# Expert products on 64x64 tiles of the array, with the expert weights loaded in an earlier phase

## The chip, the cores and the metric

The kernel runs on one core of a Trainium2 chip, as one program. The metric is the device time of one execution in microseconds (us), the median of the runs that were timed. All data are float32. The engines are named as in the profile: PE (TensorE matmul), PEld (TensorE weight load), DVE (VectorE), ACT (ScalarE), POOL (GpSimd) and SP (SyncE, which here only issues DMAs).

## The reference, cut to what matters

The model first runs a Fourier operator on 128 images of 64 x 64 (four layers; this takes the first two thirds of the span), joins 32 text rows to each, and goes on with a batch B = 128 of T = 96 tokens of D = 64 features. An attention with a recurrent state follows, and then a mixture of experts, which is what the change is about:

```
shared = gelu(x @ W1s + b1s) @ W2s + b2s
rw     = softmax(x @ Wr);  topw, topi = top_k(rw, 2);  topw /= sum(topw)
mask   = sum(one_hot(topi, 8) * topw)                 # weight of each expert for each token, mostly 0
h      = gelu(einsum('bsd,edf->bsef', x, W1p) + b1p)  # 8 experts, 64 -> 256
priv   = einsum('bsef,efd->bsed', h, W2p) + b2p       # 256 -> 64
out    = h_in + shared + einsum('bsed,bse->bsd', priv, mask)
```

The kernel computes all 8 experts for all tokens and multiplies each hidden value by its expert's weight before the second product, so that the second products of the shared expert and of the 8 private ones add up in one sum. The biases b2s and b2p have been added to `h2` by the phase before.

## The kernel before

The program is a row of phases, each with its own block of instruction streams, one for every engine, and a barrier of all engines behind it (`end_phase`, L244). `tokens` (L2132) calls them in this order: `token_norm_phase`, `update_phase`, `decay_phase`, `attention_phase`, `gate_phase`, `expert_phase`. Inside a phase the engines are ordered by semaphores alone, and each engine runs its own list in the order written. No planner sets the order.

`update_phase` (L1391) computes, for 16 groups of 8 batch entries, relu(e @ Dx.T) and its sums over channels; PE, ACT and DVE work, and SP has nothing to do until all sums are there (L1488), when it stores them.

`expert_phase` (L1955) takes the 12288 tokens in 32 blocks of 4 batch entries, that is 384 tokens (`CT`). Features or hidden units stand on the partitions, tokens along the free axis. Expert 0 is the shared one, experts 1 to 8 are the private ones. The lists of the engines:

- SP (L1992) loads W1 (the same weights twice, on partitions 0 to 63 and 64 to 127) and two copies of a 64 x 64 unit matrix. Then for each block i, two blocks ahead of its use (two buffers): the input `et` twice (L2008, the same 64 rows on both halves of the partitions; the buffer is free when block i - 2 has made its last hidden product), the mask (L2011: 8 rows of 384 weights, each broadcast to all 128 partitions, 1.5 MB; free when block i - 2 has made its last masked multiplication), and the store of block i - 2 (L2003).
- ACT (L2023) loads W2 and the two biases b1 by 11 DMAs, waits for them, and then takes the gelu with bias of 18 tiles a block (two for each of the 9 experts, 128 hidden units x 384 tokens) from four PSUM buffers `ps_h` into a ring of six SBUF tiles `ht`.
- DVE (L2045) multiplies the 16 tiles of the private experts by their mask, in place. Behind tile 6 of a block (the first of expert 3) it copies the finished sum of the block before out of PSUM (`totals`, L2047), behind tile 10 it adds the turned result to `h2` (`rows`, L2052).
- PE (L2077) makes, for each expert e, `hidden` (L2078): two products of 64 x 128 weights with the 384 tokens, one on each half of the rows of the array; and `outputs` (L2089), two experts later: two products of 128 x 64 weights, one on each half of the columns of the array, whose sums stay in PSUM over all 9 experts (upper and lower 64 partitions hold one half of the hidden units each). So hidden(e) and outputs(e - 2) take turns. Behind outputs(2) of the next block comes `turn` (L2102): four products with the unit matrices that add the two halves and turn the sum to tokens on partitions.

In float32 each matmul is two weight loads and two matmul records of the profile. `hidden` waits for ACT two experts back, `outputs` for DVE, `turn` for `totals`; such a wait stands on the first weight load behind it.

Of the kernel before, what the change touches and what calls it, by code (L numbers as in the profile page):

```python
# [12 lines left out]
P = 128  # L13
# [8 lines left out]
CH = 512  # L22
# [1367 lines left out]

def update_phase(nc, sems, W, usum):  # L1391

# [3 lines left out]
    with ExitStack() as ctx:  # L1396
# [557 lines left out]

def expert_phase(nc, sems, W, d, out, e2t_dram, gates):  # L1955

# [12 lines left out]
    n, CT = B // NB, NB * T  # L1969
    F = 2 * P  # L1970
    TILES = 2 * (E + 1)
    with ExitStack() as ctx:
        def sb(name, shape, dt=F32):
            return ctx.enter_context(nc.sbuf_tensor("x_" + name, shape, dt))

        w1 = sb("w1", [P, E + 1, F])
        w2 = sb("w2", [P, E + 1, 2, D])
        b1 = sb("b1", [P, E + 1, 2])
# [4 lines left out]
        units = sb("units", [P, D])  # L1983
# [8 lines left out]
        def _(eng):  # L1992
            for half in range(2):
                rows = slice(D * half, D * half + D)
                eng.dma_start(w1[rows, 0, :], d["W1s"]).then_inc(s.w_in, 16)
                eng.dma_start(w1[rows, 1:, :], d["W1p"].rearrange("e d f -> d e f")).then_inc(s.w_in, 16)
            for half in range(2):
                eng.dma_start(units[D * half:D * half + D, :], d["eye"][0:D, 0:D]).then_inc(s.const_in, 16)
            ov = out.rearrange("(n b) t d -> n t b d", b=NB)
# [22 lines left out]
        @block.scalar  # L2022
        def _(act):  # L2023
            act.dma_start(w2[:, 0], d["W2s"].rearrange("(t p) d -> p t d", p=P)).then_inc(s.w_tmp, 16)  # L2024
            for e in range(E):
                act.dma_start(w2[:, 1 + e], d["W2p"][e].rearrange("(t p) d -> p t d", p=P)).then_inc(s.w_tmp, 16)  # L2026
            with nc.allow_non_contiguous_dma("biases to partitions"):
                act.dma_start(b1[:, 0, :], d["b1s"].rearrange("(t p) -> p t", p=P)).then_inc(s.w_tmp, 16)  # L2028
                act.dma_start(b1[:, 1:, :].rearrange("p e t -> p (e t)"),
                              d["b1p"].rearrange("e (t p) -> p (e t)", p=P)).then_inc(s.w_tmp, 16)  # L2030
            act.wait_ge(s.w_tmp, 16 * 11)
# [12 lines left out]
        @block.vector  # L2044
        def _(dve):  # L2045
            ve = nc.vector
            def totals(i, par):  # L2047
                dve.wait_ge(s.fx_done, (E + 1) * (i + 1))
                at_least(dve, s.um_done, i)
                ve.tensor_copy(total[:, :], ps_e[par][:, 0:CT]).then_inc(s.s_ready, 1)  # L2050

            def rows(i, par, r):  # L2052
                dve.wait_ge(s.um_done, i + 1)
                if not (isinstance(i, int) and i < 2):
                    dve.wait_ge(o_out[par], 16 * r)
                ve.tensor_tensor(res[:, par], W["h2"][:, bass.ds(NB * i, NB), :],  # L2056
                                 ps_r[:, 0:NB * D].rearrange("p (b d) -> p b d", b=NB), ALU.add).then_inc(s.uo_ready, 1)

# [18 lines left out]
        def _(pe):  # L2077
            def hidden(i, par, r, e):  # L2078
# [3 lines left out]
                if not (isinstance(i, int) and i == 0 and e < 2):  # L2082
                    pe.wait_ge(s.a_ready, t - 2)
                for half in range(2):
                    rows = slice(D * half, D * half + D)
                    nc.tensor.matmul(ps_h[(2 * par + 2 * e + half) % 4][:, 0:CT], w1[rows, e, P * half:P * half + P],  # L2086
                                     et[rows, par, :], start=True, stop=True).then_inc(s.fy_done, 1)

            def outputs(i, par, e):  # L2089

                if e == 0:
                    pe.wait_ge(s.a_ready, TILES * i + 2)
                    at_least(pe, s.s_ready, i - 1)
                else:
                    pe.wait_ge(s.t_ready, 2 * E * i + 2 * e)
                for half in range(2):
                    ins = nc.tensor.matmul(ps_e[par][D * half:D * half + D, 0:CT], w2[:, e, half, :],  # L2097
                                           ht[:, (2 * e + half) % 6, :], start=(e == 0), stop=(e == E),
                                           skip_group_check=True)
                ins.then_inc(s.fx_done, 1)  # L2100

            def turn(i):  # L2102
                pe.wait_ge(s.s_ready, i + 1)
                at_least(pe, s.uo_ready, i)
                for b in range(NB):
                    ins = nc.tensor.matmul(ps_r[:, D * b:D * b + D], total[:, T * b:T * b + T], units[:, :],  # L2106
                                           start=True, stop=True)
                ins.then_inc(s.um_done, 1)

            def body(i, par, r, last):  # L2110

                later = not (isinstance(i, int) and i == 0)
                for e in range(E + 1):
# [5 lines left out]
                    if e == 4 and later:  # L2119
                        turn(i - 1)  # L2120
                if last:
                    outputs(i, par, E - 1)
                    outputs(i, par, E)
                    turn(i)

            pe.wait_ge(s.w_tmp, 16 * 11)
            pe.wait_ge(s.w_in, 64)
            pe.wait_ge(s.const_in, 32)
            walk(pe, n, body)


def tokens(nc, ctx, sems, d, h_img, out):  # L2132
# [12 lines left out]
    W = {"gate": sb("gate", [T, B, 8]), "Wr": sb("Wr", [D, 8]), "eye": sb("eye", [P, P]), "h2": sb("h2", [T, B, D])}  # L2145
    W["e"] = W["h2"]
    with nc.Block() as block:
        @block.sync
# [5 lines left out]
    with ExitStack() as c:  # L2154
# [4 lines left out]
        W["x"] = sb("x", [P, 2, B * T], c)  # L2159
        update_phase(nc, sems, W, usum)  # L2160
        end_phase(nc, sems)
# [5 lines left out]
    end_phase(nc, sems)  # L2167
    expert_phase(nc, sems, W, d, out, e2t_dram, gates)
    end_phase(nc, sems)
# [35 lines left out]
```

## Time and profile before

| | us |
|---|---|
| median of 3 runs | 3385.28 (3376.81 to 3389.48) |
| span of the profiled execution, first to last instruction | 3381.9 |
| PE busy | 2785.4 (82%) |
| DVE busy | 2119.0 (63%) |
| ACT busy | 1400.7 (41%) |
| POOL busy | 638.6 (19%) |

The profile gives the one profiled execution by its span; which of the three times was taken nearest to it, it does not say. The busy shares are means over stages of different kinds. The expert phase is the last one: it begins at about 2842 us of the span and runs to its end, some 540 us, 16% of the whole. Times in rows are us from the start of the span. A group of rows of the timeline gives start, length, engine, line, operation, names and shapes, and how many instructions have been merged; a PE shape of 64*128 is a weight tile of 64 rows and 128 columns of the array.

### The profile page before, as it was taken

To read this page: it belongs to the slowest core of one execution; us is meant where nothing else is said; L and a number is where in the kernel's file an instruction comes from. 1 tells how busy PE (TensorE), PEld (TensorE's weight loads), DVE (VectorE), ACT (ScalarE), POOL (GpSimd) and SP (SyncE) were. 2 spreads that over 40 slices of the span, in tenths; PEclk is the share of its full clock that TensorE was granted. 3 is DMA by queue.
4 is the path that set the end of the run, shared out by engine and by line. 5 is a ranking of instruction groups with operands and counts; after the bars stand their busy time and mean duration, and the time that the engine had idled before them with its cause. 6 is when DMAs were issued, how large, how long until landed. Compare 5 with 4: busy or idle time off the path is not lost. (4 is left out here: it accounts for less than half of the span.)

```text
span 3381.9 us, 104377 instructions
## 1 busy us (share of the span) xinstructions
PE 2785.4 (82%) x45316; PEld 1477.3 (44%) x45316; DVE 2119.0 (63%) x3067; ACT 1400.7 (41%) x2298; POOL 638.6 (19%) x806
## 2 busy tenths in 40 slices
PE   3589999988999999699999975825488852999999
PEld 1245555544555555355555531202266640333333
DVE  4567777766787777667777761035467653555555
ACT  2545555545555555445555541011011110666665
POOL 3003332110233311014341100000145520000000
PEclk9779989888999999899999997967777766999999
DMA  5066666654888887288888745951122203566775
GB/s 164 18 153 147 142 139 145 139 138 128 264 266 259 249 253 201 93 269 256 253 258 257 242 143 218 430 140 38 54 62 65 67 18 68 96 120 119 120 120 91
DMA packets 243990, 541.22 MB, mean 160 GB/s; under 512 B 77857, under 2 KB 124705, under 8 KB 229953
## 3 DMA queue, kind: packets, MB, share of 16 engines
q1 hardware_dynamic: 229664, 527.43, 56.8%
q10 hardware_dynamic: 13920, 7.72, 1.1%
q8 instruction: 336, 5.51, 0.6%
q14 instruction: 70, 0.57, 0.1%
HBM read 320.28 MB, written 214.78 MB: 158 GB/s over the span
## 5 line engine op out<-in xcount | busy, mean ns | idle before, releaser
L838 ACT ACTIVATE p_v<-p_ps,k_scale_bias 128x1024 f32<-128x1024 f32 x384 | 446.6, 1201 | 635.3 <-PE p_ps L947 635.1
L707 DVE STREAM_TRANSPOSE p_t<-p_ps 128x1024 f32<-128x1024 f32 x192 | 363.7, 1968 | 305.8 <-PE p_ps L700 305.4
L822 POOL COPY k_xm<-p_sp 64x288 f32<-64x288 f32 x384 | 268.8, 700 | 1453.4 <-DVE p_sp L301 1436.7
L947 PEld LDWEIGHTS p_ps<-k_idfty,p_t 64*128 64x128 f32 x6144 | 403.6, 206 | 182.5 <-issue 182.5
L845 ACT ACTIVATE p_ps<-p_ps 128x1024 f32<-128x1024 f32 x384 | 388.3, 1011 | 168.3 <-PE p_ps L963 167.9
L947 PE MATMUL p_ps<-k_idfty,p_t 64*128 64x128 f32 x6144 | 445.8, 299 | 14.7 <-issue 14.7
L291 DVE STREAM_TRANSPOSE p_vt<-p_v 128x1024 f32<-128x1024 f32 x384 | 448.2, 1208 | 0.0
L2065 DVE TENSOR_TENSOR x_ht<-x_ht,x_mask 128x384 f32<-128x384 f32 x512 | 268.6, 556 | 247.2 <-ACT x_ht L2039 244.2
L2039 ACT ACTIVATE x_ht<-x_ph,x_b 128x384 f32<-128x384 f32 x576 | 303.3, 578 | 195.3 <-PE x_ph L2086 195.3
L938 PE MATMUL p_ps<-p_v,k_wbd 32*32 32x512 f32 x4096 | 298.2, 607 | 21.7 <-DVE p_t L707 10.4
L2086 PE MATMUL x_ph<-x_et,x_w 64*128 64x384 f32 x1152 | 266.3, 540 | 35.7 <-DMA x_b<-in_L_ffn_b1p_dram 34.5
L2097 PE MATMUL x_pe<-x_ht,x_w 128*64 128x384 f32 x1152 | 249.9, 513 | 0.3 <-DVE x_ht L2065 0.3
L963 PE MATMUL p_ps<-p_v,k_wbd 32*32 32x512 f32 x6144 | 239.7, 602 | 11.0 <-DVE p_sp L301 1.1
L296 DVE STREAM_TRANSPOSE p_at<-p_ps 128x1024 f32<-128x1024 f32 x192 | 224.7, 1209 | 31.3 <-PE p_ps L269 31.3
L269 PE MATMUL p_ps<-p_vt,k_dfty 32*32 32x512 f32 x6144 | 227.9, 602 | 18.0 <-ACT p_v L838 4.6
L280 PE MATMUL p_ps<-p_at,k_dftx 32*64 32x192 f32 x6144 | 174.1, 349 | 21.6 <-DVE p_at L296 15.5
L2086 PEld LDWEIGHTS x_ph<-x_et,x_w 64*128 64x128 f32 x1152 | 87.7, 186 | 192.9 <-ACT x_ht L2039 153.1
L700 PE MATMUL p_ps<-p_yt,k_idftx 64*64 64x192 f32 x3072 | 152.8, 338 | 10.8 <-DVE p_yt L719 10.8
L938 PEld LDWEIGHTS p_ps<-p_v,k_wbd 32*32 32x32 f32 x4096 | 75.4, 103 | 193.4 <-issue 83.3
L938 PE MATMUL p_ps<-p_v,k_pwbd 4*32 4x512 f32 x2048 | 148.6, 610 | 10.1 <-issue 8.7
L301 DVE STREAM_TRANSPOSE p_sp<-p_ps 128x768 f32<-128x768 f32 x96 | 94.4, 983 | 95.8 <-PE p_ps L280 95.8
L280 PEld LDWEIGHTS p_ps<-p_at,k_dftx 32*64 32x64 f32 x6144 | 129.9, 141 | 49.9 <-issue 36.6
(298 smaller groups left out, 3114.3 us busy)
## 6 DMA issues: line engine op xcount, KB each, us to landing
field<-p_v SPq DMA_DIRECT2D x768, 256.0 KB, 4.6
p_v<-field SPq DMA_DIRECT2D x64, 2048.0 KB
x_mask<-expert_weights SPq DMA_DIRECT2D x32, 1536.0 KB, 13.9
l_v<-field SPq DMA_DIRECT2D x16, 2048.0 KB, 25.9
k_xm<-field SPq DMA_DIRECT2D x12, 2048.0 KB, 24.7
k_mixw<-in_L_tok_fw_dram SPq DMA_DIRECT2D x16, 1152.0 KB, 10.4
at_cf<-state_coefficients SPq DMA_DIRECT2D x32, 384.0 KB
k_mixw<-field SPq DMA_DIRECT2D x4, 2048.0 KB, 23.7
```

Of the source, the lines that this page charges most:

```text
L280: ins = nc.tensor.matmul(ps[64 * j:64 * j + 64, g, 0:6 * C], K["dftx"][rows, s, t, :], at[rows, s, :, 16 * t + 6 * j:16 * t + 6 * j + 6], ...
L291: return nc.vector.transpose(cols(vt), cols(px.rearrange("p (g m) -> p g m", g=G)))
L707: return nc.vector.transpose(st[:, q].rearrange("p x c -> p c x"), ps[:, 2 * q:2 * q + 2, :].rearrange("p j (m c) -> p c j m", c=C))
L822: nc.gpsimd.tensor_copy(view[64 * k:64 * k + 64, :, j, :, G * i:G * i + G], sp[64 * j:64 * j + 64, :, :, 16 * k:16 * k + M1].rearrange("p ...
L838: nc.scalar.activation(field[:, 2 * q:2 * q + 2, CH * half:CH * half + CH], ps[:, e, 2 * q:2 * q + 2, :], ACT.Relu, bias=bias, scale=scale ...
L845: nc.scalar.activation(ps[:, e, 2 * q:2 * q + 2, :], ps[:, e, 2 * q:2 * q + 2, :], ACT.Square, accum_out=K["zs"][:, at:at + 1]).then_inc(s ...
L938: nc.tensor.matmul(ps[C * a:C * a + C, e, g, :], weights[rows, C * g:C * g + C], v[rows, b, col:col + CH], start=True, stop=False, skip_gr ...
L947: ins = nc.tensor.matmul(ps[:, e, 2 * q + h, col:col + 128], lines, K["idfty"][rows, :], start=False, stop=True, skip_group_check=True)
L2039: nc.scalar.activation(ht[:, j % 6, :], ps_h[(2 * par + j) % 4][:, 0:CT], ACT.Gelu, bias=b1[:, j // 2, j % 2:j % 2 + 1]).then_inc(s.a_read ...
L2065: ve.tensor_tensor(h, h, mask[:, par, j // 2 - 1, :], ALU.mult).then_inc(s.t_ready, 1)
L2086: nc.tensor.matmul(ps_h[(2 * par + 2 * e + half) % 4][:, 0:CT], w1[rows, e, P * half:P * half + P], et[rows, par, :], start=True, stop=Tru ...
L2097: ins = nc.tensor.matmul(ps_e[par][D * half:D * half + D, 0:CT], w2[:, e, half, :], ht[:, (2 * e + half) % 6, :], start=(e == 0), stop=(e ...
```

## The change

The hidden products are cut once more, in their 128 output columns: four products of 64 x 64 weights per expert, each on its own quarter of the array. The second products are cut once more in their 128 contracted rows: again four products of 64 x 64 weights, with the two row halves summed apart, in two PSUM banks (`ps_e[:, par, c]`, c = 0 and 1). DVE's `totals` adds the two sums by one more operation. The turned result goes into the last 128 columns of the same banks, so `ps_r` is gone, and its reuse is guarded by `uo_ready` in `outputs`. The waits of `hidden` and `outputs` now stand on a `nop` ahead of the products. The loads of W1, the units, W2 and the biases have moved to SP in `update_phase`, as 17 DMAs ahead of its wait; ACT issues none.

```diff
+def expert_weights(nc, eng, X, d, done):
+    for half in range(2):
+        rows = slice(D * half, D * half + D)
+        eng.dma_start(X["w1"][rows, 0, :], d["W1s"]).then_inc(done, 16)
+        eng.dma_start(X["w1"][rows, 1:, :], d["W1p"].rearrange("e d f -> d e f")).then_inc(done, 16)
+        eng.dma_start(X["units"][rows, :], d["eye"][0:D, 0:D]).then_inc(done, 16)
+    eng.dma_start(X["w2"][:, 0], d["W2s"].rearrange("(t p) d -> p t d", p=P)).then_inc(done, 16)
+    for e in range(E):
+        eng.dma_start(X["w2"][:, 1 + e], d["W2p"][e].rearrange("(t p) d -> p t d", p=P)).then_inc(done, 16)
...
@@ update_phase, block.sync @@
+            loaded = expert_weights(nc, eng, X, d, s.w_in)
             eng.wait_ge(s.sp_ready, n // 2)
...
             eng.wait_ge(s.y_out0, 64)
+            eng.wait_ge(s.w_in, loaded)
@@ expert_phase @@
-        ps_e = [ctx.enter_context(nc.psum_tensor(f"x_pe{b}", [P, CH], F32)) for b in range(2)]
-        ps_r = ctx.enter_context(nc.psum_tensor("x_pr", [T, CH], F32))
+        ps_e = ctx.enter_context(nc.psum_tensor("x_pe", [P, 2, 2, CH], F32))
             def totals(i, par):
-                ve.tensor_copy(total[:, :], ps_e[par][:, 0:CT]).then_inc(s.s_ready, 1)
+                ve.tensor_copy(total[:, :], ps_e[:, par, 0, 0:CT]).then_inc(s.tt_done, 1)
+                dve.wait_ge(s.tt_done, i + 1)
+                ve.tensor_tensor(total[:, :], total[:, :], ps_e[:, par, 1, 0:CT], ALU.add).then_inc(s.s_ready, 1)
             def hidden(i, par, r, e):
-                for half in range(2):
-                    rows = slice(D * half, D * half + D)
-                    nc.tensor.matmul(ps_h[(2 * par + 2 * e + half) % 4][:, 0:CT], w1[rows, e, P * half:P * half + P],
-                                     et[rows, par, :], start=True, stop=True).then_inc(s.fy_done, 1)
+                pe.nop(nofuse=True)
+                for c in range(2):
+                    for half in range(2):
+                        rows, at = slice(D * half, D * half + D), P * half + D * c
+                        ins = nc.tensor.matmul(ps_h[(2 * par + 2 * e + half) % 4][D * c:D * c + D, 0:CT], w1[rows, e, at:at + D],
+                                               et[rows, par, :], start=True, stop=True)
+                        if c == 1:
+                            ins.then_inc(s.fy_done, 1)
             def outputs(i, par, e):
-                    at_least(pe, s.s_ready, i - 1)
+                    at_least(pe, s.uo_ready, i - 1)
...
+                pe.nop(nofuse=True)
                 for half in range(2):
-                    ins = nc.tensor.matmul(ps_e[par][D * half:D * half + D, 0:CT], w2[:, e, half, :],
-                                           ht[:, (2 * e + half) % 6, :], start=(e == 0), stop=(e == E),
-                                           skip_group_check=True)
+                    for c in range(2):
+                        rows = slice(D * c, D * c + D)
+                        ins = nc.tensor.matmul(ps_e[D * half:D * half + D, par, c, 0:CT], w2[rows, e, half, :],
+                                               ht[rows, (2 * e + half) % 6, :], start=(e == 0), stop=(e == E),
+                                               skip_group_check=True)
```

## Rows read from the trace of the kernel before

**Rows 1.** The page, part 4: the chain that ended last, by line.
```profile
PE x_ph L2086 7%; PE x_pe L2097 7%; PE x_pr L2106 1%; DMA x_b<-in_L_ffn_b1p_dram 1%; ACTq L2026 0%; ACT x_ht L2039 0%; ACT L2039 0%; DVE x_ht L2065 0%; ACTq L2028 0%; DVE x_total L2050 0%; ACTq L2024 0%; DVE x_res L2056 0%
```
**Rows 2.** Busy us (and instructions) of each engine, clock, DMA share, GB/s; expert phase.
```profile
2890.00:3370.00 480.00, 480.00 (x2465) 161.44 (x2464) 277.46 (x553) 291.66 (x555) 0.00 (x0) 1.00 0.67 117
```
**Rows 3.** Timeline of two stretches within a block of the expert phase.
```profile
3100.90 0.56 DVE L2065 TENSOR_TENSOR x_ht<-x_ht,x_mask 128x384 f32<-128x384 f32 x1 [0.69 <-ACT x_ht L2039]
...
3101.37 0.55 DVE L2050 COPY x_total<-x_pe 128x384 f32<-128x384 f32 x1
...
3102.54 0.89 PE L2106 MATMUL x_pr<-x_units,x_total 128*96 128x64 f32 x8
...
3103.36 0.92 PE L2086 MATMUL x_ph<-x_et,x_w 64*128 64x384 f32 x4
...
3106.64 0.92 PE L2086 MATMUL x_ph<-x_et,x_w 64*128 64x384 f32 x4
...
3107.49 0.87 PE L2097 MATMUL x_pe<-x_ht,x_w 128*64 128x384 f32 x4
3107.67 1.05 ACT L2039 ACTIVATE x_ht<-x_ph,x_b 128x384 f32<-128x384 f32 x2 [0.59 <-PE x_ph L2086]
3108.28 1.03 DVE L2065 TENSOR_TENSOR x_ht<-x_ht,x_mask 128x384 f32<-128x384 f32 x2 [0.61 <-ACT x_ht L2039]
...
3108.29 0.92 PE L2086 MATMUL x_ph<-x_et,x_w 64*128 64x384 f32 x4
```
**Rows 4.** PE's timeline: the turn of the next block.
```profile
3118.14 0.89 PE L2106 MATMUL x_pr<-x_units,x_total 128*96 128x64 f32 x8
```
**Rows 5.** Groups by line, 2890 to 3370: count, busy us, mean ns, idle before and releaser.
```profile
L2039 ACT ACTIVATE x_ht<-x_ph,x_b 128x384 f32<-128x384 f32 x555 | 292.4, 578 | 188.3 <-PE x_ph L2086 188.3
L2065 DVE TENSOR_TENSOR x_ht<-x_ht,x_mask 128x384 f32<-128x384 f32 x492 | 258.2, 556 | 201.8 <-ACT x_ht L2039 198.8
...
L2050 DVE COPY x_total<-x_pe 128x384 f32<-128x384 f32 x31 | 17.1, 551 | 0.0
```
**Rows 6.** Timeline, the last products: two `outputs` with nothing between them.
```profile
3374.28 1.51 PE L2097 MATMUL x_pe<-x_ht,x_w 128*64 128x384 f32 x8
```
**Rows 7.** Timeline of an image layer: 64x64 tiles, four at once.
```profile
1909.90 1.18 PEld L700 LDWEIGHTS p_ps<-p_yt,k_idftx 64*64 64x64 f32 x32
1909.90 1.53 PE L700 MATMUL p_ps<-p_yt,k_idftx 64*64 64x192 f32 x32
```
**Rows 8.** PE's timeline of an image layer: two groups of one shape, a nop between.
```profile
1913.28 0.59 PE L938 MATMUL p_ps<-p_v,k_wbd 32*32 32x512 f32 x1
1913.30 0.69 PE L269 MATMUL p_ps<-p_vt,k_dfty 32*32 32x512 f32 x7
```
**Rows 9.** As rows 2: a block's stream, then the phase's start.
```profile
3110.40:3125.00 14.60, 14.60 (x78) 4.94 (x76) 8.56 (x18) 8.52 (x17) 0.00 (x0) 1.00 0.64 128
...
2853.00:2863.00 10.00, 0.00 (x0) 0.00 (x0) 0.00 (x0) 0.00 (x0) 0.00 (x0) 0.50 0.76 195
2863.00:2873.50 10.50, 0.00 (x0) 0.00 (x0) 0.00 (x0) 0.00 (x0) 0.00 (x0) 0.50 0.79 132
```
**Rows 10.** Line L2011, the mask's DMA: last line of its view.
```profile
DMA to landing us min/median/max: 13.2/13.9/24.1
```
**Rows 11.** The chain that ended last, at the expert phase's start.
```profile
2842.38 0.46 ACTq L2024
...
2848.32 25.43 DMA x_b<-in_L_ffn_b1p_dram
```
**Rows 12.** Timeline at the start: first masked multiplications, outputs of expert 1.
```profile
2878.46 1.03 DVE L2065 TENSOR_TENSOR x_ht<-x_ht,x_mask 128x384 f32<-128x384 f32 x2 [37.85 <-ACT x_ht L2039]
...
2882.57 0.87 PE L2097 MATMUL x_pe<-x_ht,x_w 128*64 128x384 f32 x4
```
**Rows 13.** As rows 2: within the update phase.
```profile
2320.00:2370.00 50.00, 42.08 (x231) 18.07 (x230) 19.94 (x41) 10.46 (x24) 0.00 (x0) 0.94 0.00 1
```
**Rows 14.** Timeline: SP's first work in the update phase.
```profile
2388.55 2.81 SPq L1493 DMA_DIRECT2D update_sums<-up_row  x4
```

More of the change, by code:

```diff
@@ L1388, in _, with update_phase @@
                 dve.sem_inc(s.aggr, 1)
-def update_phase(nc, sems, W, usum):
+def expert_weights(nc, eng, X, d, done):
+    D = d["Wr"].shape[0]
+    E = X["w1"].shape[1] - 1
+    for half in range(2):
[6 more added lines that the diff above has]
+        eng.dma_start(X["w2"][:, 1 + e], d["W2p"][e].rearrange("(t p) d -> p t d", p=P)).then_inc(done, 16)
+    with nc.allow_non_contiguous_dma("biases to partitions"):
+        eng.dma_start(X["b1"][:, 0, :], d["b1s"].rearrange("(t p) -> p t", p=P)).then_inc(done, 16)
+        eng.dma_start(X["b1"][:, 1:, :].rearrange("p e t -> p (e t)"), d["b1p"].rearrange("e (t p) -> p (e t)", p=P)).then_inc(done, 16)
+    return 16 * (6 + 1 + E + 2)
+def update_phase(nc, sems, W, X, d, usum):
     s = sems
@@ L1952, in _, with expert_phase @@
                         .then_inc(s.st_done, 1)
-def expert_phase(nc, sems, W, d, out, e2t_dram, gates):
+def expert_phase(nc, sems, W, X, out, e2t_dram, gates):
     s = sems
@@ L1974, in sb @@
             return ctx.enter_context(nc.sbuf_tensor("x_" + name, shape, dt))
-        w1 = sb("w1", [P, E + 1, F])
-        w2 = sb("w2", [P, E + 1, 2, D])
-        b1 = sb("b1", [P, E + 1, 2])
+        w1, w2, b1, units = X["w1"], X["w2"], X["b1"], X["units"]
         et = sb("et", [P, 2, CT])
@@ L1992, in _ @@
         def _(eng):
-            for half in range(2):
-                rows = slice(D * half, D * half + D)
[L1995 to L1998, printed above, removed]
             ov = out.rearrange("(n b) t d -> n t b d", b=NB)
@@ L2023, in _ @@
         def _(act):
[L2024 to L2031, printed above, removed]
             def body(i, par, r, last):
@@ L2055, in rows @@
                     dve.wait_ge(o_out[par], 16 * r)
-                ve.tensor_tensor(res[:, par], W["h2"][:, bass.ds(NB * i, NB), :],
-                                 ps_r[:, 0:NB * D].rearrange("p (b d) -> p b d", b=NB), ALU.add).then_inc(s.uo_ready, 1)
+                ve.tensor_tensor(res[:, par].rearrange("p (c b) d -> p c b d", c=2),
+                                 W["h2"][:, bass.ds(NB * i, NB), :].rearrange("p (c b) d -> p c b d", c=2),
+                                 ps_e[0:T, par, :, CT:].rearrange("p c (b d) -> p c b d", d=D), ALU.add).then_inc(s.uo_ready, 1)
             def body(i, par, r, last):
@@ L2083, in hidden @@
                     pe.wait_ge(s.a_ready, t - 2)
-                for half in range(2):
-                    rows = slice(D * half, D * half + D)
-                    nc.tensor.matmul(ps_h[(2 * par + 2 * e + half) % 4][:, 0:CT], w1[rows, e, P * half:P * half + P],
-                                     et[rows, par, :], start=True, stop=True).then_inc(s.fy_done, 1)
+                pe.nop(nofuse=True)
[6 more added lines that the diff above has]
+                            ins.then_inc(s.fy_done, 1)
             def outputs(i, par, e):
@@ L2092, in outputs, with turn @@
                     pe.wait_ge(s.a_ready, TILES * i + 2)
-                    at_least(pe, s.s_ready, i - 1)
+                    at_least(pe, s.uo_ready, i - 1)
                 else:
                     pe.wait_ge(s.t_ready, 2 * E * i + 2 * e)
+                pe.nop(nofuse=True)
                 for half in range(2):
-                    ins = nc.tensor.matmul(ps_e[par][D * half:D * half + D, 0:CT], w2[:, e, half, :],
-                                           ht[:, (2 * e + half) % 6, :], start=(e == 0), stop=(e == E),
-                                           skip_group_check=True)
+                    for c in range(2):
[3 more added lines that the diff above has]
+                                               skip_group_check=True)
                 ins.then_inc(s.fx_done, 1)
-            def turn(i):
+            def turn(i, par):
                 pe.wait_ge(s.s_ready, i + 1)
-                at_least(pe, s.uo_ready, i)
                 for b in range(NB):
-                    ins = nc.tensor.matmul(ps_r[:, D * b:D * b + D], total[:, T * b:T * b + T], units[:, :],
+                    ins = nc.tensor.matmul(ps_e[0:T, par, b // 2, CT + D * (b % 2):CT + D * (b % 2) + D], total[:, T * b:T * b + T], units[:, :],
                                            start=True, stop=True)
@@ L2119, in body @@
                     if e == 4 and later:
-                        turn(i - 1)
+                        turn(i - 1, 1 - par)
                 if last:
@@ L2123, in body @@
                     outputs(i, par, E)
[L2124 to L2128, printed above, removed]
+                    turn(i, par)
             walk(pe, n, body)
@@ L2146, in tokens @@
     W["e"] = W["h2"]
+    E, F = d["W1p"].shape[0], d["W1p"].shape[2]
+    X = {"w1": sb("w1", [P, E + 1, F]), "w2": sb("w2", [P, E + 1, 2, D]), "b1": sb("b1", [P, E + 1, 2]), "units": sb("units", [P, D])}
     with nc.Block() as block:
@@ L2159, in tokens @@
         W["x"] = sb("x", [P, 2, B * T], c)
-        update_phase(nc, sems, W, usum)
+        update_phase(nc, sems, W, X, d, usum)
         end_phase(nc, sems)
@@ L2167, in tokens @@
     end_phase(nc, sems)
-    expert_phase(nc, sems, W, d, out, e2t_dram, gates)
+    expert_phase(nc, sems, W, X, out, e2t_dram, gates)
     end_phase(nc, sems)
```

2 lines of the change are left out of this document (removed).

## The prediction

> **What bounds the kernel now.** I read the chain of waits first: the end of the program hangs on PE's two expert products, with 7% of the span each, the turn with 1%, and 1% of waiting for the bias DMA [rows 1]. Then the busy times by stretch: from 2890 to 3370 us PE is busy in all 480.00 us, at full clock, ACT in 292, DVE in 277, the DMA engines in 0.67 [rows 2]. So this phase is PE's, and the timeline says how it is spent: a `hidden` starts at 3106.64, the `outputs` behind it at 3107.49, the next `hidden` at 3108.29, that is 0.85 + 0.80 = 1.65 us an expert; a turn takes 3103.36 - 3102.54 = 0.82 us [rows 3]. From turn to turn it is 15.60 us [rows 3, 4], and 9 x 1.65 + 0.82 = 15.7 gives that within rounding. Ahead of it PE is idle until the last bias has landed: 25.43 us for that DMA, and 31.4 us from the phase's first DMA at 2842.38 [rows 11].
>
> **The change part by part.** *Streaming.* Two `outputs` of one shape back to back take 1.51 us [rows 6], one alone 0.87 [rows 3]: the second costs 0.64. That is 384 columns on a full array, two records after each other. Four 64x64 tiles fill the array just as two half-array tiles do, so the streaming stays 0.64 us a product group; the cut into more matmuls doubles the records and brings no columns down. What goes is the rest, 0.85 + 0.80 - 2 x 0.64 = 0.37 us an expert, which stands wherever the shape changes between 64*128 and 128*64, and not between equal shapes [rows 3, 6]. It is the end of one shape's stream before the next may start, and the first weight load, which lies open behind it.
>
> *Do four tiles keep the pace?* An image layer does this: 32 records of 192 columns on 64*64 tiles in 1.53 us, 32 weight loads within 1.18 us of the same time [rows 7]. That is 8 sets of four; at half the columns a set should stream 0.16 us, 1.28 in all, and 0.25 is left for the first load and the last result. So loads of the same tile lie beside its running matmul. *Does the nop cost?* Line 938 has such a nop ahead of it and so has 269, both 32*32; their records start 0.02 us apart and overlap [rows 8]. I take 0 for a seam; the other end is an open first load in each of 18 seams, by the 0.37 above at most half of 0.19, say 0.05 each, 0.9 a block; below zero there is nothing to gain.
>
> *PE's block then:* 18 x 0.64 = 11.5 us, 0.82 for the turn, and two changes of shape around it, of which one is in the 0.82 already: another 0.15. That is 12.5 us before waits.
>
> *Waits that come late now.* ACT needs 292.4/555 x 18 = 9.5 us a block and DVE 258.2/492 x 16 = 8.4, with the copy 0.55, the new addition 0.55 (same shape, as the copy) and the `rows` operation about 0.4: 9.9 us [rows 5]. Both stay under 12.5. In latency: gelu starts 1.03 us behind its `hidden`, the multiplication 0.61 behind that and takes 1.03 for two tiles [rows 3]: 2.7 us, and `outputs` of that expert comes 2 x 1.28 + 0.64 = 3.2 us behind its `hidden`. It fits, with 0.5 us to spare. The turn doesn't: it stands behind outputs(2), at 5 x 1.28 = 6.4 us of the block (+0.1). DVE takes the totals behind the first tile of expert 3: `hidden`(3) at 3.84, gelu at +0.95 (no open load), multiplication at +0.61, totals 0.47 later (3100.90 to 3101.37 [rows 3]), so the copy runs 5.87 to 6.42 and the addition, which must wait for it, to 7.0. PE stands about 0.6 us; before, the copy ended at 3101.92 and the turn started at 3102.54, by PE alone [rows 3]. Behind PE's wait stand hidden(5) and outputs(3), which DVE's late tile would have held anyway. Compute bound: 12.5 + 0.6 = 13.1, call it 13.2 us a block.
>
> *What is late next: the mask.* Each block brings 1.57 MB of mask, 0.2 of inputs and 0.1 of output. This stream now takes 14.6 us at 128 GB/s, and then pauses for a microsecond [rows 9]; a mask lands 13.9 us after its issue [rows 10]. Its issue waits for the last multiplication two blocks back, and it is needed about 13.2 + 1.5 us later: the latency just fits, but the streams of two blocks then follow without the pause. At 128 GB/s they would need 14.6 us a block. At the phase's start, where requests were piled up, (195 x 10 + 132 x 10.5)/20.5 = 163 GB/s passed [rows 9], 11.5 us a block. No row shows a piled-up stream beside working engines. The 14.6 hold a head and a tail of half a microsecond each, in which few packets move and which a stream without pause covers; I take 13.6 us, nearer to the row with the engines at work. The block is the larger, 13.6. Gain: 31 x (15.6 - 13.6) = 62 us.
>
> *Loads moved.* In the update phase the DMA engines are idle (0.00, 2320 to 2370) [rows 13] and SP has nothing to do until 2388.55 [rows 14]. 17 issues of 0.59 us ((2848.32 - 2842.38)/10 [rows 11]) are 10 us on SP; with all the landings the same loads took 31.4 us, two masks among them. Begun at 2320 at the latest, they end by 2352: 36 us of cover. PE, ACT and DVE of that phase read no DMA. Cost 0; without the cover it would be all 31 us. In the expert phase nothing is ahead of the inputs: mask 0 goes out at 2842.4 + 2 x 0.6 = 2843.6 and lands 13.9 later [rows 10], at 2857.5, while PE makes hidden(0) to (3) at half clock and ACT loads its table, all hidden. Outputs(1) then follows at about 2858.6 instead of 2882.57 [rows 12]: 24 us. PE has cooled meanwhile, where before it was warm by 2882.57 (0.87 us a group there); some 4.6 us of half-clock work come again, 2.5 us. Start: -21.5. At the end the second totals operation costs +0.5.
>
> *Sum:* -62 - 21.5 + 0.5 = -83. The span of 3381.9 becomes 3299; the median of the runs lies 3.4 above that span, 3385.3 becomes **3302 us**.
>
> **A rule that speaks against it.** Rows 7 show weight loads inside the matmuls' time. The Trainium skill ("TensorE: Matmul & The Clock Gate", Part 3, The mechanism) says that a weight load overlaps running matmuls only when it goes to another row group. Here all row groups are in use, so by that rule every set's load would lie open. By that rule rows 7 could not be; I give it the small chance of the slower rival below.
>
> **The rivals.**
> *Compute alone binds* (the piled-up stream reaches over 141 GB/s): 13.2 us a block, -74 - 21 = 3290. For it: the 163 of rows 9. Against: the engines stood still there.
> *The mask binds at today's rate or a little better*, 14.1 to 14.6 us a block: -46 to -31, with the start 3332 to 3318. For it: 128 GB/s in a stretch in which the DMA engines were 0.64 busy, so that they didn't set the rate [rows 9], and then a backlog need not help. The same time comes out if the nops lay open 18 loads (14.1).
> *Slower:* each set of four opens its weight loads. A group has two sets; 32 loads take 1.18 us in rows 7, 4 some 0.15, so a group takes 0.64 + 0.3 = 0.94, a block 17 + 0.8 = 17.8, +68 - 21: 3432. It decides for slower from 0.11 us a set on. Against it: rows 7, where eight sets leave 0.25 us in all.
> *The start doesn't move* (the first mask as late as the biases were, 24.1 us at most from its issue [rows 10], or the moved loads hold up the update's end): 10 to 21 us less gain, 3312 to 3323.
>
> **How the numbers follow.** Forecast (13.4 to 13.9 us a block, 3295 to 3312) 0.45; compute alone 0.25; mask at 14.1 to 14.6 or open nops 0.20; start not moved 0.06; slower 0.03; no change by some cancelling, 0.01. The range, from compute alone with a shorter stall at the turn (13.0 us: 3283) to a mask at 14.5 us: 3282 to 3330. Half a per cent, 17 us, is about what a measurement tells from no change here. Faster 0.96, same 0.01, slower 0.03.
>
> **What would show it.** Right: `hidden` and `outputs` start 0.64 us apart with PE gapless, 64*64 x8 in each; the turn idles about 0.6 us for line 2050's successor; one wait a block on DVE for the mask, with DMA busy without a pause; first products at 2845, first multiplication near 2857; update phase as long as before. Wrong: groups of 0.7 us or more (loads or nops), turns under 13.2 us apart, the mask in no wait, or waits of PE for ACT in every expert.

## The result, and the profile after

The changed kernel took 3299.27 us (median of 4 runs, 3287.43 to 3308.56) against 3387.38 for the kernel before, timed beside it: a ratio of 0.9747, 95% interval 0.9712 to 0.9781. In two later series its median was 3291.22 and 3291.01 us. The forecast was 3302, within 3282 to 3330, so time and direction came out. The mechanism that the forecast took to be the likeliest did not: a block of the expert phase takes 13.14 us, not 13.6, and it is PE's waits and products that set it, not the stream of masks.

The chain of waits that ended last in the changed kernel (the page, part 4) answers to [rows 1]: PE's two products have 4% of the span each, the bias DMA is gone, and a mask has come in.

```profile
PE x_ph L2091 4%; PE x_pe L2107 4%; DMA x_mask<-expert_weights 2%; PE x_pe L2115 1%; ACT x_ht L2039 1%; DVE x_total L2052 0%; DVE x_total L2050 0%; DVE x_ht L2068 0%; SPq L2017 0%; DVEq L123 0%; DVE x_res L2058 0%; DVEq L2066 0%; ACTq L2038 0%; ACTq L134 0%; ACTq L2036 0%
```

These are three stretches of the changed kernel (columns as in [rows 2]): the update phase, in which the DMA engines were idle before [rows 13], the start of the expert phase, and its steady part. In the last of them PE is busy in 390.56 of 405 us, where it was busy without a pause [rows 2], and the DMA engines carry 139 GB/s instead of 117.

```profile
2320.00:2370.00 50.00, 42.07 (x232) 18.06 (x230) 19.95 (x41) 10.46 (x24) 0.00 (x0) 0.94 0.19 30
2843.00:2858.00 15.00, 5.00 (x40) 1.76 (x40) 0.00 (x0) 4.70 (x9) 0.00 (x0) 0.73 0.62 138
2870.00:3275.00 405.00, 390.56 (x4680) 190.89 (x4676) 287.88 (x585) 291.22 (x554) 0.00 (x0) 1.00 0.83 139
```

The timeline of the changed kernel around a turn answers to [rows 3, 4]. `outputs` and `hidden` start 0.64 to 0.65 us apart (2944.29, 2944.94, 2945.58, 2946.23), so 1.29 us an expert and not 1.65. Their weight loads begin while the group before still runs: those of the group at 2944.94 are at 2944.62. The turn waits 0.48 us for DVE's new addition. From turn to turn it is 2955.91 - 2942.78 = 13.13 us.

```profile
2941.58 0.55 DVE L2050 COPY x_total<-x_pe 128x384 f32<-128x384 f32 x1
...
2942.17 0.56 DVE L2052 TENSOR_TENSOR x_total<-x_total,x_pe 128x384 f32<-128x384 f32 x1
...
2942.78 0.89 PE L2115 MATMUL x_pe<-w_units,x_total 128*96 128x64 f32 x8 [0.48 <-DVE x_total L2052]
...
2943.60 0.88 PE L2091 MATMUL x_ph<-x_et,w_w 64*64 64x384 f32 x8
...
2944.29 0.82 PE L2107 MATMUL x_pe<-x_ht,w_w 64*64 64x384 f32 x8
...
2944.62 0.15 PEld L2091 LDWEIGHTS x_ph<-x_et,w_w 64*64 64x64 f32 x4 [0.17 <-issue]
2944.94 0.82 PE L2091 MATMUL x_ph<-x_et,w_w 64*64 64x384 f32 x8
...
2945.58 0.82 PE L2107 MATMUL x_pe<-x_ht,w_w 64*64 64x384 f32 x8
...
2946.23 0.83 PE L2091 MATMUL x_ph<-x_et,w_w 64*64 64x384 f32 x8
...
2955.91 0.89 PE L2115 MATMUL x_pe<-w_units,x_total 128*96 128x64 f32 x8 [0.47 <-DVE x_total L2052]
```

The waits of the changed kernel from 2870 to 3275 us (who waited for whom, us in total, times, longest): DVE waits 16 times for a mask, but of these 31.5 us only 1.0 reaches PE. The 13.4 at the turn are the new totals operation.

```profile
PEld x_pe L2115 <- DVE x_total L2052: 34.1, 31, 1.1
DVE x_ht L2068 <- DMA x_mask<-expert_weights: 31.5, 16, 2.7
PE x_pe L2115 <- DVE x_total L2052: 13.4, 31, 0.5
PE x_pe L2107 <- DVE x_ht L2068: 1.0, 2, 0.6
```

The timeline of its start: the mask goes out at 2843.51 and the first masked multiplication is at 2858.43 (2878.46 before [rows 12]). PE had reached full clock by 2849.00 (`outputs` of expert 0, 0.83 us for eight records), made one more `hidden` and stood for 9.13 us. Outputs(1) comes at 2859.61, at half clock: the granted clock is 0.50 from 2859.00 to 2865.50 us, and eight records take 1.56 us. From 2865.76 on they take 0.83 again.

```profile
2842.30 1.15 SPq L2017 DMA_DIRECT2D x_et<-expert_inputs  x2
...
2843.51 0.58 SPq L2020 DMA_DIRECT2D x_mask<-expert_weights  x1
...
2845.47 3.71 PE L2091 MATMUL x_ph<-x_et,w_w 64*64 64x384 f32 x24 [6.24 <-DMA x_et<-expert_inputs]
...
2858.43 2.90 DVE L2068 TENSOR_TENSOR x_ht<-x_ht,x_mask 128x384 f32<-128x384 f32 x6 [17.88 <-DMA x_mask<-expert_weights]
...
2859.61 1.56 PE L2107 MATMUL x_pe<-x_ht,w_w 64*64 64x384 f32 x8 [9.13 <-DVE x_ht L2068]
...
2865.76 0.83 PE L2091 MATMUL x_ph<-x_et,w_w 64*64 64x384 f32 x8
```

Times of whole runs differ by 10 us and more within each kernel. The traces show where much of it is: the expert phase's first DMA stands at 2842.3 us here and at 2824.8 in another profile of the very same kernel. The comparisons below therefore give the length of the expert phase too, from its first DMA to the end of the span, read from the one trace of each row. The small-mask kernels leave out seven of a mask's eight rows from the third block on, so their output is not the reference's; they are there to measure.

| kernel | ratio to the kernel before (95%) | median us | expert phase us | usual turn to turn us |
|---|---|---|---|---|
| before | 1 | 3378 to 3387 by series | 539.5 | 15.60 |
| the change | 0.9747 (0.9712 to 0.9781) | 3299.27 | 443.3 | 13.14 |
| again | 0.9730 (0.9709 to 0.9752) | 3291.22 | 447.7 | 13.14 |
| again | 0.9731 (0.9703 to 0.9759) | 3291.01 | 440.7 | 13.14 |
| preload alone | 0.9946 (0.9924 to 0.9968) | 3367.45 | 519.1 | 15.60 |
| tiles alone | 0.9798 (0.9768 to 0.9827) | 3314.11 | 462.1 | 13.14 |
| change, `hidden` as before | 0.9964 (0.9941 to 0.9987) | 3371.12 | 522.9 | 15.69 |
| change, small mask | 0.9718 (0.9692 to 0.9744) | 3290.26 | 440.3 | 13.14 |
| change, turn later | 0.9758 (0.9739 to 0.9777) | 3302.06 | 451.1 | 13.22 |
| the same, mask in halves | 0.9738 (0.9714 to 0.9762) | 3297.78 | 442.6 | 13.22 |
| change, totals and turn later | 0.9723 (0.9695 to 0.9752) | 3290.64 | 445.2 | 12.59 to 13.53 |
| the same, small mask | 0.9661 (0.9630 to 0.9692) | 3271.44 | 425.4 | 12.59 |
| the same, mask in halves | 0.9671 (0.9641 to 0.9700) | 3268.73 | 427.4 | 12.59 |

### The profile page after: what moved, and what is told of

It reads as the page before. It is cut to its first block and busy times, and to the rows that moved or that the text cites. A ratio compares the mean times of both kernels' runs of the same rounds, so it can differ in the third digit from the quotient of the medians.

```text
span 3285.6 us, 109526 instructions
## 1 busy us (share of the span) xinstructions
PE 2691.4 (82%) x47620; PEld 1506.3 (46%) x47620; DVE 2128.4 (65%) x3099; ACT 1400.1 (43%) x2298; POOL 638.5 (19%) x806
## 5 line engine op out<-in xcount | busy, mean ns | idle before, releaser
L2039 ACT ACTIVATE x_ht<-x_ph,w_b 128x384 f32<-128x384 f32 x576 | 303.2, 578 | 131.6 <-PE x_ph L2091 131.6
L2068 DVE TENSOR_TENSOR x_ht<-x_ht,x_mask 128x384 f32<-128x384 f32 x512 | 261.7, 555 | 138.8 <-ACT x_ht L2039 89.1
L938 PE MATMUL p_ps<-p_v,k_wbd 32*32 32x512 f32 x4096 | 298.4, 609 | 19.0 <-DVE p_t L707 10.3
L2107 PE MATMUL x_pe<-x_ht,w_w 64*64 64x384 f32 x2304 | 239.9, 486 | 10.6 <-DVE x_ht L2068 10.6
L2091 PE MATMUL x_ph<-x_et,w_w 64*64 64x384 f32 x2304 | 242.0, 490 | 6.2 <-DMA x_et<-expert_inputs 6.2
L296 DVE STREAM_TRANSPOSE p_at<-p_ps 128x1024 f32<-128x1024 f32 x192 | 224.3, 1205 | 31.5 <-PE p_ps L269 31.5
L280 PE MATMUL p_ps<-p_at,k_dftx 32*64 32x192 f32 x6144 | 170.5, 346 | 21.6 <-DVE p_at L296 15.5
L719 DVE STREAM_TRANSPOSE p_yt<-k_xm 128x768 f32<-128x768 f32 x96 | 145.1, 1512 | 0.0
```

The lines of the kernel that those rows point to most:

```text
L280: ins = nc.tensor.matmul(ps[64 * j:64 * j + 64, g, 0:6 * C], K["dftx"][rows, s, t, :], at[rows, s, :, 16 * t + 6 * j:16 * t + 6 * j + 6], ...
L938: nc.tensor.matmul(ps[C * a:C * a + C, e, g, :], weights[rows, C * g:C * g + C], v[rows, b, col:col + CH], start=True, stop=False, skip_gr ...
L2068: ve.tensor_tensor(h, h, mask[:, par, j // 2 - 1, :], ALU.mult).then_inc(s.t_ready, 1)
L2091: ins = nc.tensor.matmul(ps_h[(2 * par + 2 * e + half) % 4][D * c:D * c + D, 0:CT], w1[rows, e, at:at + D], et[rows, par, :], start=True, ...
L2107: ins = nc.tensor.matmul(ps_e[D * half:D * half + D, par, c, 0:CT], w2[rows, e, half, :], ht[rows, (2 * e + half) % 6, :], start=(e == 0), ...
```

## The experiments

There were three questions: do the two gains add up, is it the change of shape or the four tiles that brought the blocks' gain, and what sets the block of 13.14 us, PE with DVE's order or the stream of masks?

**The preload alone.** The kernel before, with its 17 loads in the update phase:

```diff
 update_phase, sync:
+            loaded = expert_weights(nc, eng, X, d, s.w_in)
             eng.wait_ge(s.sp_ready, n // 2)
 expert_phase, sync, scalar and tensor:
...
-            pe.wait_ge(s.w_tmp, 16 * 11)
-            pe.wait_ge(s.w_in, 64)
-            pe.wait_ge(s.const_in, 32)
```

> The kernel before, with the loads of the expert weights moved into the update phase and nothing else changed. Theory (two gains that add up: the block of the expert phase 15.60 to 13.14 us, and the start): the turns stay 15.60 us apart and the time falls by the start alone, 19 to 22 us, ratio to the kernel before about 0.994. Rival (the preload is worth nothing by itself, since the first mask lands late in any case): less than 8 us, with the first masked multiplication at the place that it has before.

Measured: ratio 0.9946, 3367.45 us, 18 under the kernel before by the ratio. The chain of its trace shows what has come in the place of the bias DMA [rows 11]:

```profile
2843.79 14.55 DMA x_mask<-expert_weights
2858.37 1.04 DVE x_ht L2067 x2
2859.45 1.55 PE x_pe L2099 x4
```

The wait of 25.43 us, which began at 2848.32, is now one of 14.55 from 2843.79 on. The first mask now sets the start, the turns stay 15.60 us apart, and the expert phase is 20.4 us shorter. The rival, under 8 us with the first masked multiplication where it was, is out: that multiplication came from 2878.46 to 2858.37.

**The tiles alone.** The changed kernel with the 17 loads, and the waits for them, where they were:

```diff
 update_phase, sync:
-            loaded = expert_weights(nc, eng, X, d, s.w_in)
...
 expert_phase, sync, scalar and tensor:
+            for half in range(2):
+                rows = slice(D * half, D * half + D)
+                eng.dma_start(w1[rows, 0, :], d["W1s"]).then_inc(s.w_in, 16)
...
+            act.dma_start(w2[:, 0], d["W2s"].rearrange("(t p) d -> p t d", p=P)).then_inc(s.w_tmp, 16)
...
+            pe.wait_ge(s.w_tmp, 16 * 11)
+            pe.wait_ge(s.w_in, 64)
+            pe.wait_ge(s.const_in, 32)
```

> The changed kernel with the expert weights loaded at the start of the expert phase, as before the change. Theory: turns 13.14 us apart, 31 x 2.46 = 76 us less than the kernel before, ratio about 0.978; the start as late as before, PE's first product some 31 us behind the phase's first DMA. Rival (without the preload the masks come later and hold the blocks): turns over 13.5 us apart, gain under 65 us.

Measured: ratio 0.9798, 3314.11 us, 68 under the kernel before by the ratio. Turns are 13.14 us apart but for one of 13.47, and PE's first product comes 31.0 us behind the phase's first DMA, both as the theory had it; the expert phase is 77.4 us shorter than before. So tiles 77.4 and preload 20.4 make 97.8 us, against the 96.2 of the change (539.5 - 443.3) in the first profile and 92 to 99 in the other two: the two gains add up. The 3.6 us beyond 30 x 2.46 lie ahead of the first turn, where the products are on the new tiles too (53.8 us from the phase's first DMA instead of 57.4).

**`hidden` on 64x128 again.**

```diff
-                for c in range(2):
-                    for half in range(2):
-                        rows, at = slice(D * half, D * half + D), P * half + D * c
-                        ins = nc.tensor.matmul(ps_h[(2 * par + 2 * e + half) % 4][D * c:D * c + D, 0:CT], w1[rows, e, at:at + D],
-                                               et[rows, par, :], start=True, stop=True)
-                        if c == 1:
-                            ins.then_inc(s.fy_done, 1)
+                for half in range(2):
+                    rows = slice(D * half, D * half + D)
+                    nc.tensor.matmul(ps_h[(2 * par + 2 * e + half) % 4][:, 0:CT], w1[rows, e, P * half:P * half + P],
+                                     et[rows, par, :], start=True, stop=True).then_inc(s.fy_done, 1)
```

> The changed kernel with hidden cut as before (two products of 64x128 weights), outputs on four 64x64 tiles; the shape changes twice per expert, as in the kernel before. Theory (the gain is the change of shape that is gone, not the four tiles): hidden and outputs take 0.85 and 0.8 us again, turns about 15.6 us apart, so the time stands about 20 us under the kernel before, ratio 0.994. Rival (four tiles at once are faster by themselves): half of the gain of the blocks stays, turns about 14.4 us apart, ratio about 0.983.

Measured: ratio 0.9964, 3371.12 us, turns 15.69 us apart, as the theory had it. PE's timeline:

```profile
3101.52 0.92 PE L2090 MATMUL x_ph<-x_et,w_w 64*128 64x384 f32 x4
3102.36 0.88 PE L2104 MATMUL x_pe<-x_ht,w_w 64*64 64x384 f32 x8
3103.17 0.92 PE L2090 MATMUL x_ph<-x_et,w_w 64*128 64x384 f32 x4
```

The groups start 0.84 and 0.81 us apart, as in [rows 3]. `outputs` on four 64x64 tiles takes just as long as it did on two 128x64 tiles while its neighbour has another shape. With both in one shape each takes 0.645. Four tiles at once bring nothing by themselves: the gain of the blocks is that PE changes shape twice a block, around the turn, and not 19 times. The traces show a part of what a change costs. Between equal shapes the loads stand 0.32 us ahead of their group; at a change the first loads start only with it (3102.36 for both here, 3107.49 for both in the kernel before). How much of the 0.18 us is the open load and how much the end of the stream before it, no run separates. Nor was the new tiling tried without the nops. They aren't enough for the gain, since this kernel has them, and [rows 6] show the 0.64 us without one.

**The change again, and with a small mask.**

> The changed kernel once more, as the measure for the kernels of this call. Theory: turns 13.14 us apart but for a few blocks that wait for a mask, 3290 to 3308 us from run to run. Rival (the prediction's forecast, that the stream of masks sets the block): most blocks over 13.4 us.

```diff
+                few = E if isinstance(i, int) and i < 2 else 1
-                eng.dma_start(mask[:, par], gates.rearrange("(o e) (n b) t -> n o e (b t)", o=1, b=NB)[i]
-                              .broadcast_to([P, E, CT])).then_inc(m_in[par], 16)
+                eng.dma_start(mask[:, par, 0:few], gates.rearrange("(o e) (n b) t -> n o e (b t)", o=1, b=NB)[i][:, 0:few]
+                              .broadcast_to([P, few, CT])).then_inc(m_in[par], 16)
```

> The changed kernel with the mask's DMA cut to one of its eight rows from the third block on (the other seven keep the values of the first two blocks, so the masked products of experts 2 to 8 are not the reference's). Theory (compute binds, and the mask takes only a block here and there): every block 13.14 us, and 1 to 15 us less than the changed kernel in the same call, with the spread between runs gone. Rival (the mask stream is what sets the block in most runs): over 15 us less, with blocks well under 13.14.

Measured: 3291.22 us for the change and 3290.26 with the small mask, ratios 0.9730 and 0.9718 with intervals that overlap for the most part. No block of the small-mask kernel is over 13.14 us, with DMA down to 38 GB/s. The full mask costs the change single blocks: 13.55 and 13.68 in the first profile, 13.39 in this one. So the forecast's stream was not the bound, and compute binds. The spread from run to run did not go either (3281.57 to 3309.31 with the small mask): that part of my expectation was wrong.

**The turn later.** If compute binds, where are the 0.6 us over the 12.5 that the forecast gave PE? The turn is put behind outputs(3):

```diff
-                    if e == 4 and later:
+                    if e == 5 and later:
                         turn(i - 1, 1 - par)
...
-                    if j == 10 and later:
+                    if j == 12 and later:
                         rows(i - 1, 1 - par, r - 1 + par)
```

> The changed kernel with the turn one expert later (behind outputs(3)) and DVE's rows behind tile 12 in place of tile 10; nothing is left out. Theory: PE's 0.47 us of waiting at the turn, and the weight loads that lie open behind it, go, some 0.6 us a block, 12.5 in place of 13.14; but the mask's stream of 1.87 MB a block at 142 GB/s needs 13.2 us, so most of the 19 us is not paid out: blocks 12.8 to 13.2 us, 0 to 10 us less. Rival (the mask has room enough): blocks 12.5 us, 19 us less. Other rival (DVE's order makes the loss come back elsewhere): no change and no mask wait.

Measured: ratio 0.9758, 3302.06 us, no gain; blocks of 13.22 us. The theory's 12.8 to 13.2 us a block and 0 to 10 us less did not come out. The last rival did, in that the loss comes back elsewhere; its "no mask wait" is not quite so, for DVE waits 8 times for a mask, 15.5 us in all, but PE waits in nearly every block for DVE's late tile instead, 28 times and 10.3 us. Of the 11 us that its median lies above the change's, the blocks explain 2; its trace has one block of 19.12 us besides (see the last section), and the rest stays open. The timeline:

```profile
3109.33 0.55 DVE L2050 COPY x_total<-x_pe 128x384 f32<-128x384 f32 x1
...
3109.87 0.82 PE L2091 MATMUL x_ph<-x_et,w_w 64*64 64x384 f32 x8
...
3109.92 0.55 DVE L2052 TENSOR_TENSOR x_total<-x_total,x_pe 128x384 f32<-128x384 f32 x1
3110.39 2.43 DVE L2068 TENSOR_TENSOR x_ht<-x_ht,x_mask 128x384 f32<-128x384 f32 x5
...
3111.09 0.88 PE L2107 MATMUL x_pe<-x_ht,w_w 64*64 64x384 f32 x8 [0.39 <-DVE x_ht L2068]
```

The two operations of the totals stand between the two tiles of expert 3 in DVE's list. Outputs(3), due at 3110.5, waits for the second tile, which DVE begins at 3110.39 only. The wait has moved by one product.

**The turn later and the mask in halves.**

```diff
+            def part(i, par, k):
+                some = slice(4 * k, 4 * k + 4)
+                eng.dma_start(mask[:, par, some], gates.rearrange("(o e) (n b) t -> n o e (b t)", o=1, b=NB)[i][:, some]
+                              .broadcast_to([P, 4, CT])).then_inc((m_in if k == 0 else m2_in)[par], 16)
             def body(i, par, r, last):
+                at_least(eng, s.t_ready, 2 * E * (i - 2) + E)
+                part(i, par, 0)
                 at_least(eng, s.fy_done, TILES * (i - 1))
...
                 at_least(eng, s.t_ready, 2 * E * (i - 1))
+                part(i, par, 1)
 vector:
                 for j in range(2, TILES):
+                    if j == 10:
+                        dve.wait_ge(m2_in[par], 16 * r + 16)
```

> The turn later as in the kernel above, and each mask loaded in two DMAs of four experts, the first issued as soon as the first half of the buffer is free, half a block earlier; nothing is left out. Theory (a mask is late by the latency from its issue, and less by what the stream can carry): 5 to 20 us less than the changed kernel, blocks 12.5 to 12.9 us. Rival (the stream's rate is the limit): as the kernel with the turn later alone, blocks about 13.1 us.

Measured: ratio 0.9738, 3297.78 us, blocks of 13.22 us and no wait for a mask between 2870 and 3270 us. The theory (12.5 to 12.9) is out. The rival's time came out, as with the turn later alone, but not its reason: with DVE's order as it is, the mask doesn't count, neither by its latency nor by its rate.

**Totals and turn later.** DVE's totals go behind tile 7, so that both tiles of expert 3 are done first:

```diff
-                    if j == 6 and later:
+                    if j == 7 and later:
                         totals(i - 1, 1 - par)
```

The turn stands behind outputs(3) and the rows behind tile 12. This was run once with the full mask, once with the small one, once with the mask in halves, beside the change once more.

> The changed kernel, as the measure for the kernels of this call: blocks of 13.14 us, the time within 3288 to 3309 us.

> The changed kernel with DVE's totals behind tile 7 in place of 6, the turn behind outputs(3) and rows behind tile 12; nothing is left out. Theory (the 0.6 us a block are the place of the totals in DVE's list: with the turn alone moved, outputs(3) waited 0.4 us for tile 7, which stood behind the totals): PE waits for DVE nowhere. What then binds is the mask's stream: blocks 12.8 to 13.2 us with waits for the mask, 0 to 10 us less than the changed kernel. Rival (the stream keeps up): blocks of 12.5 us, 19 us less. Other rival (another order of DVE has the same cost at another place): 13.1 us and no wait for the mask.

> The same order with the mask's DMA cut to one of its eight rows from the third block on (the masked products of experts 2 to 8 are not the reference's). Theory: PE's own bound, blocks of 12.5 us, 19 us less than the changed kernel; what the kernel with the full mask stands above it is the price of the mask's stream. Rival (PE has further open loads or waits): 12.8 us or more.

> The same order with the full mask in two halves, the first issued half a block earlier. Theory (rate-bound stream): as with the mask in one DMA, within 3 us. Rival (latency-bound mask): blocks at 12.5 us, up to 19 us less than the changed kernel.

Measured, in this order: 0.9731, 0.9723, 0.9661 and 0.9671. The change again has one block of 13.34 us and otherwise 13.14, and its lowest run, 3267.31 us, lies under the range that I had given it. With the small mask every block is 12.59 us and the median 20 us under the change, as the theory had it: that is PE's bound, 18 x 0.645 + 0.82 + 0.15. With the full mask in one DMA the blocks run from 12.59 to 13.53, mean 12.82 over the 28 between the first and the last two; the theory of the mask as the next bound holds here, but not its reason. The stretches from 2900 to 3240 us of the three kernels, full mask, small mask, halves:

```profile
2900.00:3240.00 340.00, 337.13 (x4023) 168.76 (x4019) 243.27 (x500) 250.71 (x478) 0.00 (x0) 1.00 0.86 145
```
```profile
2900.00:3240.00 340.00, 340.00 (x4112) 166.89 (x4108) 252.10 (x514) 255.45 (x486) 0.00 (x0) 1.00 0.14 39
```
```profile
2900.00:3240.00 340.00, 339.06 (x4096) 167.03 (x4092) 251.02 (x512) 254.58 (x485) 0.00 (x0) 1.00 0.85 148
```

In halves the same bytes pass at 148 GB/s, and DVE waits for no mask; in one DMA it waits 16 times, 36.4 us in all, and PE in turn stands 6 times for DVE. In halves one block is 13.76 us long, in which PE waits 0.94 us for its inputs, and the first 14.57. This is that wait in the kernel with one DMA, and the landing times of the mask's DMA in the two kernels, one DMA and halves:

```profile
3110.73 2.90 DVE L2068 TENSOR_TENSOR x_ht<-x_ht,x_mask 128x384 f32<-128x384 f32 x6 [2.66 <-DMA x_mask<-expert_weights]
```
```profile
DMA to landing us min/median/max: 13.5/14.6/21.5
```
```profile
DMA to landing us min/median/max: 8.6/8.9/16.2
```

14.6 us from issue to landing, with the issue bound to the last use two blocks back, do not fit into a block of 12.59 and the 1.5 us until the next use. The limit was the time from issue to landing, not the rate of the stream, and the rival was right. Most of that time is the transfer itself (14.6 us whole, 8.9 a half, 3.2 for one row), and the halves are both shorter and, the first, issued half a block earlier; which of the two does more was not tried. The halves are the version that beats both kernels: 3268.73 us, 3.3% under the kernel before. Against the change in the same series its interval (0.9641 to 0.9700) lies under that of the change (0.9703 to 0.9759), 0.6% less; the interval of the kernel with one DMA (0.9695 to 0.9752) still overlaps with its own, by 0.0005.

## Why the prediction came out, and which step of it failed

By the profiled executions the change is 3285.57 - 3381.94 = -96.4 us: the first turn comes 34.4 us behind the phase's first DMA instead of 57.4 (-23.0), from the first turn to the last it is 404.5 us instead of 477.8 (-73.3), and behind that 4.4 instead of 4.3 (+0.1).

- *Streaming 0.64 us a group on four tiles, seams and nops at 0*: right. Groups start 0.645 us apart. The slower rival, each set of four opening its loads, is refuted by the same rows: the loads lie 0.3 us ahead of their group. The Trainium skill's sentence that a load overlaps running matmuls only in another row group ("TensorE: Matmul & The Clock Gate", Part 3, The mechanism) does not hold in this trace, where all row groups were in use. The same section also lets a load run ahead when it goes to a background weight buffer, and the loads here run ahead as that would allow.
- *What goes is the change of shape*: right, 0.18 us a change, and shown by `hidden` on 64x128 alone, which brings the blocks back to 15.69.
- *PE's block of 12.5 us before waits*: 12.59, once DVE's order and the mask are out of the way.
- *The turn stands 0.6 us for the second totals operation*: right; 0.48 us of idle matmul, and 13.14 - 12.59 = 0.55 us in all. The prediction said that outputs(3) would be held by DVE's late tile anyway; it is, and so a later turn alone gives nothing.
- *The mask's stream sets the block at 13.6*: wrong. This is the step that failed, "At 128 GB/s they would need 14.6 us a block ... I take 13.6 us, nearer to the row with the engines at work". 128 GB/s was the rate of a stream that waits for its next request, not the rate that the engines can carry; with the requests close behind one another it was 139 in the change, and 148 where the blocks asked for that much. The small mask settles it: with 38 GB/s the block is 13.14 us all the same. One of the prediction's own signs of being wrong came up, turns under 13.2 us apart; and in place of a wait for the mask in every block there were 16, of which 1.0 us reached PE. The term was -62 and is -73.3. (It also counts 31 blocks, but the last of the 31 distances is a short one, 9.92 us before and 9.54 after, so 13.6 would have given some -60.) The rival *compute alone binds*, 13.2 us a block and 3290 us with a chance of 0.25, had the mechanism, and its time is that of two of the three medians, 3291. The row from the phase's start, 163 GB/s, was the better guide, and "the engines stood still there" no reason against it.
- *Loads moved at no cost*: right. SP issues them from 2316.7 to 2327.6, the phase's store stands at 2388.54 (2388.55 before [rows 14]), and DMA traffic of 30 GB/s there holds up nobody.
- *Start -21.5*: -23.0 to the first turn, of which the preload alone makes 20.4; the mask is what the start waits for, forecast at 2857.5 and seen at 2858.4. The half-clock work that comes again was 5.9 us, longer than the 4.6 of the forecast.
- *End +0.5*: +0.1 behind the last turn.

That 3302 lies so near to the first median (3299) is luck: the block was put 0.46 us too long, some 14 us over the phase, and the runs of that series lay 8 us above those of the two later ones. The profiled execution was the fastest of its four, 3287.43 us; by it the change is 96 us, by the ratio of the medians 86.

## What to carry to other kernels

Where PE goes back and forth between two shapes of weight tile, look at the distance of group starts against the same groups back to back: the difference, here 0.18 us a change, came back whole when both products were cut to one shape, and not by packing more tiles. For a transfer that starts when its buffer is free, two numbers are needed: the time from issue to landing, and the rate under load. The rate seen in a stream that pauses bounds neither, and cutting the buffer so that half of it comes free earlier tells them apart. An operation put into a list of an engine costs both those who wait for it and those who wait for what stands behind it; move the two together.

## What was not expected of the hardware

- A group of 384 columns that fills the array takes 0.80 to 0.85 us when its neighbour has another shape, on two tiles of 64x128 or 128x64 or on four of 64x64 alike.
- With a broadcast of eight rows of 1.5 KB to 128 partitions in every block, the DMA engines moved 128 GB/s where the requests had pauses between them [rows 9], and 139 to 148 GB/s where the next request was out before the last had landed, both beside working engines.
- In some executions PE stands once or twice for some microseconds, and the profile shows nothing that it waits for ("issue"). In the second profile of the change this is in the middle of a group, behind the first turn:

```profile
2879.39 0.81 PE L2107 MATMUL x_pe<-x_ht,w_w 64*64 64x384 f32 x5
2883.79 0.54 PE L2107 MATMUL x_pe<-x_ht,w_w 64*64 64x384 f32 x2 [3.59 <-issue]
```

That block took 18.93 us instead of 13.14; the rest of the loss is that PE comes back at half clock (granted 0.64 from 2884 to 2888 us). The kernel with totals and turn later has two such blocks (19.34 and 19.39 us), the one with the turn later alone has one (19.12); the two with the mask in halves have shorter stops at the same place (first blocks of 14.24 and 14.57 us). The first and third profile of the change have none, nor have the tiles alone or the two kernels with the small mask. That the mask's transfers hold up the loading of instructions would fit, but kernels with the full mask and no stop speak against it as the whole cause; it was not tried. In the profiles such stops are a part of the 22 us by which the medians of the mask in one DMA and in halves differ, of which the blocks' mean explains 6.
- The length of the phases ahead of the expert phase differs by up to 30 us between profiles of kernels that are the same up to there; why stays open.
